# A vision tower's routed stage: lanes free with the table, tables sent sooner, outputs kept in fetched rows

## Chip, cores and metric

One Trainium2 chip, one of its cores. The time is the device time of one execution in microseconds; the kernel's figure is the median of three runs. In the profile PE is TensorE (PEld its weight loads), DVE VectorE, ACT ScalarE, POOL GpSimd, SP SyncE; L12 is line 12 of the kernel before.

## What is computed

Two layers of a small vision tower over 832 tokens (32 images, 26 positions, 256 features), all in float32. The change is in the last block, a mixture of 32 experts of which each token uses one, plus one shared expert:

```python
h = _L0_tok_ref(x, L0_tok_W)                    # patches, + class token
h = h + _L0_attn_ref(_layernorm(h), ...)
h = h + _L0_ffn_ref(_layernorm(h), ...)
h = h + _L1_attn_ref(_layernorm(h), ...)
h = h + _L1_ffn_ref(_layernorm(h), ...)         # the block that changes

# _L1_ffn_ref
shared_out = silu(x @ shared_gate_w) * (x @ shared_up_w) @ shared_down_w
logits = x @ gate_w
topk_ids = argmax(logits); scores = sigmoid(max(logits))
xs = x * scores
order = argsort(topk_ids)                       # tokens sorted by expert
g, u = grouped(xs[order], routed_gate_w), grouped(xs[order], routed_up_w)
d = grouped(silu(g) * u, routed_down_w)
return shared_out + d[argsort(order)]
```

## The kernel before

Every engine has its own hand-written stream, ordered by semaphores. Tokens are eight groups of 104. `x3T` holds the normalised tokens transposed (832 columns). The names that the change touches:

- **Memory.** One big tile, the arena, holds eight weight slots (one expert each, 1536 KB), behind them four *lanes*, behind them the shared expert's hidden values `hidT` and weights. `kz`, which also held `x3T`, and `zB`, which receives the shared silu, lie inside the area of the lanes. `cols3` is another tile (`qT`, `kT`, `xA` are its thirds, `quad` is all of it).
- **Routing.** VectorE derives from the logits the sorted slot of each token and two sets of records: *feeds* (which expert to load into which slot, and how many quads must have been copied before that slot is free) and *quads* (where the four weight sets of a quad lie, and how many loads must have landed). TensorE turns columns into rows for them (L607, `feeds_done`; L612 and L613, `table_done`), VectorE casts them into `table` (L1166 `feeds_table`, L1184 `table_ready`), and each engine loads its records into registers (`entry`, `weights_of`, `more_quads`), with bounds checked at run time.
- **Shared expert, up.** `shared_up(0..7)` on TensorE, a silu on ScalarE into `zB`, `hidden(0..7)` on VectorE into `hidT`; hand-placed between the routing steps. `shared_up(n)` waits for `hidden(n-2)`.
- **Tokens.** POOL scatters the scaled rows to `sorted_x` in memory (L1301). SP fetches windows of 128 rows back into `xw`: window 0, windows 1 and 2, windows 3 to 6 (`WINDOW_PARTS`); POOL fetches window 7.
- **Quads.** 128 sorted rows make a quad of four strips of 32 rows, each strip with one expert. In pass q TensorE does the gate and up strips of quad q (L628), the transpose of window q+1 (L620), some groups of `shared_down`, the down strips of quad q-1 (L641) and the transposes of quad q's hidden values (L634). ScalarE does the silu and evictions, VectorE the product (L1189) and the eviction of outputs (L1192). Before strips of quad q+1 can run, its weights are copied from slots into lanes: eight copies of 128x1024 on VectorE (L1195 to L1206), four on ScalarE (L824). Copies wait for `loaded`; SP waits for `copied_dve` and `copied_act` to reuse a slot.
- **Feeds.** SP keeps two loads in flight: it waits for the older one, raises `loaded`, waits until the slot is free, issues the next (L307).
- **Outputs.** `shared_rows(g)` adds the shared output to h, POOL stores it (L1317); when all eight groups are stored, POOL adds the quads' rows with indirect DMAs (L1310). The rows lie in a ring of four buffers `yw`, and VectorE waits for addition q-5 before it reuses one. `aim_static` computes the target rows of seven quads.
- **Last loop.** Passes 0 to 7 are written out. A loop of `more_quads` rounds (at least one; here one) does the down strips and addition of quad 7 and also the next quad, which is empty here. TensorE in it: down strips, wait for the window, transpose, gate strips, up strips, transposes. The end of the kernel waits for all engines.

## Time and profile before

| | |
|---|---|
| median of 3 runs | 354.5 us (353.39 to 355.84) |
| profiled execution | 352.22 us, span 350.4 us |
| TensorE, VectorE, ScalarE busy | 300.3, 206.3, 134.8 us |
| granted clock of TensorE, mean | 0.951 |
| expert loads after the routing | 14 of 1536 KB, issued 255.2 to 318.4 |
| stage from the first quad to the end | 263.8 to 350.4 |

The span runs from the first to the last instruction of the profiled execution; the execution's own time is 1.8 us more. All rows below give times from the start of the span. Busy shares are means over stages with different limits, so the stretch of the change is read by its waits, its chain and its timelines.

### The profile page before, as it was taken

How to read it: one execution, taken by the hardware profiler on the slowest of the kernel's cores; microseconds unless marked ns; L12 is line 12 of the kernel's file. 1: busy time of each engine (PE TensorE's matmuls, PEld its weight loads, DVE VectorE, ACT ScalarE, POOL GpSimd, SP SyncE). 2: the span in 40 equal slices, each digit the busy share in tenths (PEclk: the TensorE clock that was granted, in tenths of full speed). 3: DMA queues.
4: the chain of work that ended last, by engine and by line, in shares of the span. 5: the costliest groups of instructions: out<-in, count | busy, mean ns of one | idle time of the engine just before them, and what ended most of it. 6: DMA issues, size and time to landing. Idle time of an engine off the chain costs nothing.

```text
span 350.4 us, 6874 instructions
## 1 busy us (share of the span) xinstructions
PE 300.3 (86%) x2484; PEld 213.8 (61%) x2484; DVE 206.3 (59%) x589; ACT 134.8 (38%) x309; POOL 56.0 (16%) x73
## 2 busy tenths in 40 slices
PE   1996979388899999999975999989899999964958
PEld 1774548277899999998963766665454555421322
DVE  0454684433465665665266699948739867645653
ACT  1021242243242242242233466529147545615650
POOL 0111000100110110110000001111711210442350
PEclk9999899879999999999997799999999999996996
DMA  7999991003364264053597200000389996899231
GB/s 291 397 435 426 410 316 48 2 0 111 131 241 151 91 239 147 34 181 129 233 353 285 85 2 2 6 4 0 86 299 395 394 354 251 336 358 397 49 46 17
DMA packets 13115, 67.73 MB, mean 193 GB/s; under 512 B 1738, under 2 KB 7322, under 8 KB 8986
## 3 DMA queue, kind: packets, MB, share of 16 engines
q1 hardware_dynamic: 11050, 64.28, 47.9%
q0 software_dynamic: 2032, 3.02, 4.1%
q8 instruction: 20, 0.33, 0.4%
q14 instruction: 13, 0.11, 0.1%
HBM read 61.38 MB, written 5.91 MB: 192 GB/s over the span
## 4 chain that ended last, share of the span: by engine, by line
PE 64%; issue 11%; DMA 10%; DVE 8%; ACT 3%; SPq 1%; DVEq 1%; POOL 1%; ACTq 0%
PE P L340 17%; PE P L460 8%; PE P L448 8%; PE P L628 7%; DMA arena<-experts_dram 7%; PE P L374 4%; PE P L484 4%; PE P L510 3%; PE P L436 2%; PE P L641 2%; DMA vrow<-sorted_x 2%; DMA arena<-patches_dram 2%; PE P L525 1%; DVE arena L996 1%; PE P L535 1%
## 5 line engine op out<-in xcount | busy, mean ns | idle before, releaser
L340 PE MATMUL P<-arena 128*104 128x256 f32 x288 | 73.5, 395 | 9.4 <-DMA arena<-patches_dram 7.1
L340 PEld LDWEIGHTS P<-arena 128*104 128x104 f32 x288 | 47.4, 176 | 22.4 <-issue 8.3
L1290 POOL TENSOR_TENSOR rstd<-var,mhalf 104x1 f32<-104x1 f32 x40 | 21.9, 548 | 210.5 <-DVE var L919 210.5
L628 PE MATMUL P<-arena,cols 128*32 128x512 f32 x288 | 37.3, 664 | 11.1 <-ACT cols L849 9.1
L824 ACT ACTIVATE arena<-arena 128x1024 f32 x31 | 31.5, 1051 | 21.2 <-SPq L325 9.1
L460 PE MATMUL P<-arena 128*128 128x104 f32 x256 | 29.9, 275 | 2.4 <-ACT arena L764 2.4
L460 PEld LDWEIGHTS P<-arena 128*128 128x128 f32 x256 | 29.7, 192 | 3.1 <-issue 1.4
L448 PEld LDWEIGHTS P<-arena 128*128 128x128 f32 x256 | 29.8, 192 | 1.2 <-issue 0.7
L448 PE MATMUL P<-arena 128*128 128x104 f32 x256 | 29.8, 275 | 0.5 <-issue 0.5
L628 PEld LDWEIGHTS P<-arena,cols 128*32 128x32 f32 x288 | 9.1, 120 | 32.6 <-issue 19.1
L764 ACT ACTIVATE arena<-P,arena 128x104 f32<-128x104 f32 x64 | 17.0, 348 | 27.7 <-PE P L448 27.7
L577 PE MATMUL P<-arena 128*128 128x416 f32 x64 | 24.1, 522 | 2.0 <-DVE arena L1107 2.0
L749 ACT ACTIVATE arena<-P,arena 128x104 f32<-128x104 f32 x16 | 6.1, 433 | 43.2 <-PE P L427 43.2
L1310 POOL DMA_INDIRECT out_dram<-cols,target x8 | 16.5, 2058 | 23.5 <-DVE cols L1192 18.0
L925 DVE TENSOR_SCALAR arena<-h,mv,rstd 104x256 f32<-104x256 f32 x24 | 9.9, 413 | 16.0 <-POOL rstd L1290 16.0
L577 PEld LDWEIGHTS P<-arena 128*128 128x128 f32 x64 | 11.6, 190 | 11.4 <-issue 8.0
L641 PE MATMUL P<-arena,cols 128*32 128x256 f32 x192 | 15.4, 381 | 1.0 <-ACT cols L852 1.0
L484 PE MATMUL P<-arena 128*128 128x104 f32 x128 | 15.6, 275 | 0.6 <-DVE arena L1017 0.6
L484 PEld LDWEIGHTS P<-arena 128*128 128x128 f32 x128 | 15.0, 192 | 0.9 <-ACT arena L775 0.8
L1189 DVE TENSOR_TENSOR cols<-cols,P 128x512 f32<-128x512 f32 x9 | 6.2, 688 | 15.2 <-PE P L628 11.0
L724 ACT ACTIVATE cols<-P 128x104 f32<-128x104 f32 x16 | 4.2, 363 | 28.0 <-PE P L358 28.0
L917 DVE BATCH_NORM_STATS2 st<-h 104x6 f32<-104x256 f32 x32 | 13.7, 428 | 1.1
(200 smaller groups left out, 480.3 us busy)
## 6 DMA issues: line engine op xcount, KB each, us to landing
arena<-experts_dram SPq DMA_DIRECT2D x22, 1536.0 KB, 8.4
arena<-experts_dram SPq DMA_DIRECT2D x8, 2048.0 KB, 12.7
arena<-patches_dram SPq DMA_DIRECT2D x4, 624.0 KB, 6.3
sorted_x<-arena SPq DMA_DIRECT2D x1, 2056.0 KB, 35.2
arena<-shared_dram SPq DMA_DIRECT2D x1, 1536.0 KB, 32.4
arena<-w_dram SPq DMA_DIRECT2D x1, 1024.0 KB, 9.8
out_dram<-arena SPq DMA_DIRECT2D x1, 1024.0 KB, 33.7
out_dram<-h POOLq DMA_DIRECT2D x8, 104.0 KB, 4.9
```

Source lines behind the costliest of these rows:

```text
L340: last = mm(P[b][0:a.shape[1], col:col + D], a, rhs(c), start=(c == 0), stop=(c == chunks - 1))
L374: last = mm(bank(n % 4, HALF), w0_s[:, w, c, m * 128:(m + 1) * 128], xA[:, c, half * HALF:(half + 1) * HALF], start=(c == 0), stop=(c == D ...
L448: last = mm(bank(3 + m // 4, 4, GT)[:, m % 4, :], w[:, c, m * 128:(m + 1) * 128], xaT[:, c, :], start=(c == 0), stop=(c == DC - 1))
L460: last = mm(P[5][:, m * GT:(m + 1) * GT], w[:, c, m * 128:(m + 1) * 128], fhT[:, c, :], start=(c == 0), stop=(c == HC - 1))
L484: last = mm(bank(6, 4, GT)[:, 2 * w + m, :], w1_s[:, w, c, m * 128:(m + 1) * 128], x2T[:, c, :], start=(c == 0), stop=(c == DC - 1))
L577: last = mm(bank(b, HALF), w[:, c, m * 128:(m + 1) * 128], x3T[:, c, half * HALF:(half + 1) * HALF], start=(c == 0), stop=(c == DC - 1))
L628: last = mm(P[b][part, :], xT[:, c, part], weights(u)[:, c * INNER:(c + 1) * INNER], start=(c == 0), stop=(c == DC - 1), tile_position=(0, ...
L641: last = mm(P[3][part, 0:D], hT[:, c * 128 + STRIP * u:c * 128 + STRIP * (u + 1)], down_of(u, parity)[:, c * D:(c + 1) * D], start=(c == 0 ...
L764: A(fhT[:, m, :], bank(3 + m // 4, 4, GT)[:, m % 4, :], ACT.Gelu, bias=bcol_s[:, B1 + HC * g + m:B1 + HC * g + m + 1])\
L824: return A(to, third(where, n), ACT.Copy)
L1290: nc.gpsimd.tensor_tensor(rstd[:, :], var[:, :], mhalf[:, :], ALU.pow).then_inc(s["rstd_ready"], 1)
L1310: pool.indirect_dma_start(out, bass.IndirectOffsetOnAxis(ap=target[:, c:c + 1], axis=0), yw[:, c % YBUFS, :], None, compute_op=ALU.add)\
```

## The change

- `x3T` moves from `kz` to `qT`, `zB` into `quad`: the lanes are no longer touched by the shared up products. VectorE and ScalarE copy quad 0's weights as soon as the table is there, with `hidden(5)`, `(6)`, `(7)` placed between VectorE's copies.
- The feed records' product goes from behind `shared_up(4)` to behind `shared_up(3)`, the quad records' from behind `shared_up(5)` to behind `shared_up(4)`; `hidden(3)` goes behind the feed cast.
- Checks of record values at run time are dropped but for one per record.
- SP issues the second feed ahead of waiting for the scatters, and then the windows.
- `shared_down(0)` and `(1)` come before the quads, then one group in passes 1 and 2, two in passes 3 and 4 (before: group 0 ahead, group 1 in pass 0, two each in passes 1 to 3).
- Outputs are evicted into the fetched rows `xw` (quad 7: `y_last`); the ring `yw` and its waits go, the additions share a semaphore; `aim_static` covers eight quads and waits for window 7.
- The last loop: ScalarE copies two gate parts, VectorE five parts, ahead of the evictions; TensorE transposes the window ahead of the down strips; POOL fetches the first such window ahead of addition 6, and each further one behind the aim, which VectorE computes behind the product; the end waits for that window.
- `sorted_x` is one block of 128 rows longer.

Left out below: the buffer view `y_last`, the block count, the single semaphore `added`, and the checks' arguments in `entry`.

```diff
@@ -35,16 +35,19 @@
 WINDOW_PARTS = (0, 1, 3)
-SORTED = (MAX_QUADS + 1) * 128
+BLOCKS = MAX_QUADS + 2
+SORTED = BLOCKS * 128
...
 SPILLS = STILL + 1
-YBUFS = 4
+SHARED_FIRST = 2
+SHARED_AT = ((), (2,), (3,), (4, 5), (6, 7), (), (), ())
...
 XROW = D + 1
+IN_TABLE = "VectorE bounds each entry when it makes the table"
@@ -133,7 +136,8 @@
         x3 = vrow[:, :, 0:D]
-        oT = x3T = kz
+        oT = kz
+        x3T = qT
@@ -156,7 +160,7 @@
         spr = flat5[:, HALF + DC * GT:HALF + 2 * DC * GT].rearrange("p (c t) -> p c t", c=DC)
-        zB = flat5[:, 0:2 * HALF].rearrange("p (a n) -> p a n", a=2)
+        zB = quad[:, 0:2 * HALF].rearrange("p (a n) -> p a n", a=2)
@@ -226,8 +230,9 @@
             row = table[0:1, at:at + QUAD] if isinstance(q, int) else table[0:1, bass.ds(at, QUAD)]
-            _, found = nc.values_load_multi_w_load_instructions(row, engines=[engine.engine], min_val=0, max_val=(SLOTS - 1) * SLOT)
-            return found[LANES], found[0:LANES]
+            _, found = nc.values_load_multi_w_load_instructions(row, engines=[engine.engine], min_val=0, max_val=(SLOTS - 1) * SLOT,
+                                                                skip_runtime_bounds_check_because=IN_TABLE)
+            return nc.s_assert_within(found[LANES], 1, EXPERTS + 1), found[0:LANES]
@@ -312,10 +318,9 @@
             second = entry(1)
+            feed(second, 1)
             sp.wait_ge(xs_sent, 16 * GROUPS)
-            window(0)
-            feed(second, 1)
-            for i in range(1, len(WINDOW_PARTS)):
+            for i in range(len(WINDOW_PARTS)):
@@ -599,19 +604,19 @@
             last.then_inc(s["prefix_done"], 1)
-            for n in range(2, 5):
+            for n in range(2, 4):
                 shared_up(n)
...
             last.then_inc(s["feeds_done"], 1)
-            shared_up(5)
+            shared_up(4)
             pe.wait_ge(s["blocks_ready"], 1)
...
             mm(records[:, :, LANES], tcol[0:64, 1:2], ident[0:64, bass.ds(LANES - 1, 16, LANES)], start=True, stop=True).then_inc(s["table_done"], 1)
-            for n in range(6, 2 * IC):
+            for n in range(5, 2 * IC):
                 shared_up(n)
@@ -650,7 +655,8 @@
-            shared_down(0)
+            for g in range(SHARED_FIRST):
+                shared_down(g)
@@ -679,11 +685,8 @@
                     next_xt(q + 1)
-                if q == 0:
-                    shared_down(1)
-                elif q <= 3:
-                    shared_down(2 * q)
-                    shared_down(2 * q + 1)
+                for g in SHARED_AT[q]:
+                    shared_down(g)
                 if q >= 1:
@@ -697,13 +700,13 @@
             with pe.Fori(0, more) as i:
+                pe.wait_ge(l_window_in, 16 * (i + 2))
+                xt(STILL).then_inc(s["l_xt_done"], 1)
                 pe.wait_ge(s["l_hT_ready"], i + 1)
...
                 down_strips(STILL % 2).then_inc(s["l_dn_done"], 1)
-                pe.wait_ge(l_window_in, 16 * (i + 2))
-                xt(STILL).then_inc(s["l_xt_done"], 1)
                 pe.wait_ge(s["l_xT_ready"], i + 1)
@@ -854,7 +857,6 @@
-            act.wait_ge(s["hid_ready"], 2 * IC)
@@ -884,16 +886,16 @@
             with act.Fori(0, more) as i:
-                act.wait_ge(s["l_ht_done"], i + 1)
-                hT_evac().then_inc(s["l_hT_ready"], 1)
                 need, where = weights_of(act, i + (STILL + 1))
...
                 copy_third(where[3], 0, gate_of(3))
+                act.wait_ge(s["l_ht_done"], i + 1)
+                hT_evac().then_inc(s["l_hT_ready"], 1)
+                act.wait_ge(s["l_xt_done"], i + 2)
+                xT_evac().then_inc(s["l_xT_ready"], 1)
                 copy_third(where[2], 1, up_of(2)).then_inc(s["l_gatew_in"], 1)
                 act.wait_ge(s["l_dn_done"], i + 1)
-                act.wait_ge(s["l_xt_done"], i + 2)
-                xT_evac().then_inc(s["l_xT_ready"], 1)
                 copy_third(where[2], 2, down_of(2, STILL % 2)).then_inc(s["copied_act"], 1)
@@ -1158,12 +1160,11 @@
             V.tensor_scalar(table[:, T_FEEDS:T_FEEDS + 1], rounds, 1.0, None, ALU.max)
-            hidden(3)
...
             V.tensor_copy(table[:, 0:T_QUAD], P[5][0:1, 288:288 + T_QUAD]).then_inc(s["feeds_table"], 1)
+            hidden(3)
@@ -1182,14 +1183,12 @@
             V.tensor_copy(table[:, T_QUAD:NTABLE], P[4][0:1, 256:256 + 16 * QUAD]).then_inc(s["table_ready"], 1)
-            hidden(5)
-            hidden(6)
...
-            def y_evac(c):
-                return V.tensor_copy(yw[:, c, :], P[3][:, 0:D])
+            def y_evac(to):
+                return V.tensor_copy(to, P[3][:, 0:D])
@@ -1212,22 +1211,27 @@
                     dve.wait_ge(part, 16)
-                live7, ids7 = live[:, :, 0:STILL], xw[:, 0:STILL, D]
-                V.tensor_scalar(live7[:, 0, :], ids7, 0.0, None, ALU.is_gt)
-                link(V.tensor_tensor(live7[:, 1, :], ids7, route[:, C_SPILL1:C_SPILL1 + STILL], ALU.subtract))
-                link(V.tensor_tensor(live7[:, 1, :], live7[:, 1, :], live7[:, 0, :], ALU.mult))
-                V.tensor_tensor(target[:, 0:STILL], live7[:, 1, :], route[:, C_SPILL:C_SPILL + STILL], ALU.add).then_inc(s["aim_ready"], 1)
+                dve.wait_ge(l_window_in, 16)
+                dve.wait_ge(s["l_added"], 16)
+                ids8 = xw[:, 0:SPILLS, D]
+                V.tensor_scalar(live[:, 0, :], ids8, 0.0, None, ALU.is_gt)
+                link(V.tensor_tensor(live[:, 1, :], ids8, route[:, C_SPILL1:C_SPILL1 + SPILLS], ALU.subtract))
+                link(V.tensor_tensor(live[:, 1, :], live[:, 1, :], live[:, 0, :], ALU.mult))
+                V.tensor_tensor(target[:, :], live[:, 1, :], route[:, C_SPILL:C_SPILL + SPILLS], ALU.add).then_inc(s["aim_ready"], 1)
...
             need, where = weights_of(dve, 0)
-            hidden(7)
-            dve.wait_ge(s["hid_ready"], 2 * IC)
             dve.wait_ge(s["loaded"], need)
+            dve.wait_ge(s["xs_scaled"], GROUPS)
             copy_gate(where).then_inc(s["gatew_in"], 1)
+            hidden(5)
             copy_up(where).then_inc(s["upw_in"], 1)
-            shared_rows(0)
+            hidden(6)
...
             need, where = weights_of(dve, 1)
+            hidden(7)
+            for g in range(SHARED_FIRST):
+                shared_rows(g)
@@ -1241,15 +1245,11 @@
                     aim_static()
-                    shared_rows(1)
-                elif q <= 3:
-                    shared_rows(2 * q)
-                    shared_rows(2 * q + 1)
+                for g in SHARED_AT[q]:
+                    shared_rows(g)
...
                     dve.wait_ge(s["dn_done"], q)
-                    if q > YBUFS:
-                        dve.wait_ge(added[q - 1 - YBUFS], 16)
-                    y_evac((q - 1) % YBUFS).then_inc(s["y_ready"], 1)
+                    y_evac(xw[:, q - 1, 0:D]).then_inc(s["y_ready"], 1)
@@ -1258,26 +1258,25 @@
             nc.vector.nop().then_inc(s["l_turn"], 1)
-            dve.wait_ge(added[STILL - YBUFS], 16)
             with dve.Fori(0, more) as i:
-                dve.wait_ge(s["l_added"], 16 * (i + 1))
-                dve.wait_ge(l_window_in, 16 * (i + 1))
+                need, where = weights_of(dve, i + (STILL + 1))
+                dve.wait_ge(s["loaded"], need)
+                copy_gate(where)
+                copy_up(where).then_inc(s["l_gatew_in"], 1)
+                dve.wait_ge(s["l_dn_done"], i + 1)
+                y_evac(y_last).then_inc(s["l_y_ready"], 1)
+                copy_down(where, STILL % 2).then_inc(s["copied_dve"], 1)
+                dve.wait_ge(s["l_sgate_ready"], i + 1)
+                dve.wait_ge(s["l_up_done"], i + 1)
+                mul().then_inc(s["l_hw_ready"], 1)
+                dve.wait_ge(l_window_in, 16 * (i + 2))
                 ids = xw[:, STILL, D:XROW]
...
                 dve.wait_ge(s["l_aimed"], i + 1)
+                dve.wait_ge(s["l_added"], 16 * (i + 2))
                 V.scalar_tensor_tensor(target[:, STILL:], live[:, 1, STILL:], live[:, 0, STILL:], route[:, C_SPILL + STILL:C_SPILL + SPILLS],
                                        ALU.mult, ALU.add).then_inc(s["l_aim_ready"], 1)
-                need, where = weights_of(dve, i + (STILL + 1))
-                dve.wait_ge(s["l_dn_done"], i + 1)
-                y_evac(STILL % YBUFS).then_inc(s["l_y_ready"], 1)
-                dve.wait_ge(s["loaded"], need)
-                copy_gate(where)
-                copy_up(where).then_inc(s["l_gatew_in"], 1)
-                copy_down(where, STILL % 2).then_inc(s["copied_dve"], 1)
-                dve.wait_ge(s["l_sgate_ready"], i + 1)
-                dve.wait_ge(s["l_up_done"], i + 1)
-                mul().then_inc(s["l_hw_ready"], 1)
@@ -1304,10 +1303,12 @@
-                pool.dma_start(xw[:, STILL, :], sorted_x[bass.ds(r * 128, 128), :]).then_inc(l_window_in, 16)
+                rows_r = slice(r * 128, (r + 1) * 128) if isinstance(r, int) else bass.ds(r * 128, 128)
+                pool.dma_start(xw[:, STILL, :], sorted_x[rows_r, :]).then_inc(l_window_in, 16)
...
             def add_rows(c, done):
-                pool.indirect_dma_start(out, bass.IndirectOffsetOnAxis(ap=target[:, c:c + 1], axis=0), yw[:, c % YBUFS, :], None, compute_op=ALU.add)\
+                y = xw[:, c, 0:D] if c < STILL else y_last
+                pool.indirect_dma_start(out, bass.IndirectOffsetOnAxis(ap=target[:, c:c + 1], axis=0), y, None, compute_op=ALU.add)\
@@ -1320,21 +1321,23 @@
                     pool.wait_ge(s["stored"], 16 * GROUPS)
+                if r == STILL - 1:
+                    pool.wait_ge(s["l_xt_done"], 1)
+                    window(STILL + 1)
                 pool.wait_ge(s["y_ready"], r + 1)
-                add_rows(r, added[r])
+                add_rows(r, added)
...
             with pool.Fori(0, more) as i:
-                pool.wait_ge(s["l_aim_ready"], i + 1)
-                pool.wait_ge(s["l_xt_done"], i + 1)
                 pool.wait_ge(s["l_turn"], i + 1)
-                window(i + (STILL + 1))
                 pool.wait_ge(s["l_y_ready"], i + 2)
...
                 add_rows(STILL, s["l_added"])
-            for r in range(STILL):
-                pool.wait_ge(added[r], 16)
-            pool.wait_ge(l_window_in, 16 * (more + 1))
+                pool.wait_ge(s["l_xt_done"], i + 2)
+                pool.wait_ge(s["l_aim_ready"], i + 1)
+                window(i + (STILL + 2))
+            pool.wait_ge(added, 16 * STILL)
+            pool.wait_ge(l_window_in, 16 * (more + 2))
             pool.wait_ge(s["l_added"], 16 * (more + 1))
```

## Rows read from the trace of the kernel before

**Rows 1.** The page, part 1: busy us, share of the span, instructions.
```profile
PE 300.3 (86%) x2484; PEld 213.8 (61%) x2484; DVE 206.3 (59%) x589; ACT 134.8 (38%) x309; POOL 56.0 (16%) x73
```

**Rows 2.** Waits, 240 to 352: waiter <- awaited: total us, times, longest.
```profile
ACT arena L824 <- SPq L325: 9.1, 1, 9.1
```

**Rows 3.** The chain that ended last, from 225: start, us, engine and line.
```profile
257.03 5.72 DMA vrow<-sorted_x
...
273.94 3.45 PE P L340 x16
...
301.44 7.44 DMA arena<-experts_dram
...
318.42 8.14 DMA arena<-experts_dram
...
329.03 3.64 PE P L628 x32
...
348.75 0.70 DVE cols L1189
```

**Rows 4.** DVE timeline, 247 to 254: start, us, engine, line, operation.
```profile
247.41 0.15 DVE L1154 TENSOR_SCALAR tcol<-own 128x1 f32<-128x1 f32 x1
...
251.48 0.25 DVE L1166 CAST table<-P 1x96 int32<-1x96 f32 x1 [1.82 <-PE P L607]
...
253.52 0.15 DVE L1177 TENSOR_SCALAR tcol<-own 128x1 f32<-128x1 f32 x1
```

**Rows 5.** PE timeline, 248 to 290: shared products, tables, first strips of quads.
```profile
248.12 3.06 PE L577 MATMUL P<-arena 128*128 128x416 f32 x8 [1.15 <-DVE arena L1107]
...
254.36 0.27 PE L612 MATMUL P<-ident,tcol 64*1 64x64 f32 x2
...
260.31 1.89 PE L340 MATMUL P<-arena 128*104 128x256 f32 x8
...
263.83 3.64 PE L628 MATMUL P<-arena,cols 128*32 128x512 f32 x32 [0.53 <-ACT cols L849]
...
269.93 3.64 PE L628 MATMUL P<-arena,cols 128*32 128x512 f32 x32
...
289.62 3.64 PE L628 MATMUL P<-arena,cols 128*32 128x512 f32 x32
```

**Rows 6.** SP timeline: issue of the first fed expert.
```profile
255.16 0.36 SPq L307 DMA_DIRECT2D arena<-experts_dram  x1
```

**Rows 7.** Windows: stretch, length, busy of PE, PEld, DVE, ACT, POOL; clock, DMA, GB/s.
```profile
270.00:284.00 14.00, 14.00 (x122) 6.59 (x123) 11.05 (x24) 7.96 (x12) 2.75 (x3) 1.00 0.98 388
301.40:326.60 25.20, 16.93 (x166) 5.97 (x162) 12.87 (x21) 10.99 (x15) 10.03 (x5) 0.86 0.96 341
341.00:349.00 8.00, 6.51 (x32) 1.39 (x32) 3.08 (x6) 1.08 (x2) 0.53 (x1) 0.57 0.16 18
```

**Rows 8.** DVE timeline, 299 to 301.3: last weight copy of quad 4.
```profile
300.56 0.69 DVE L1206 COPY arena<-arena 128x1024 f32 x1
```

**Rows 9.** ACT, DVE, POOL, PE timelines of the last pass, 334 to 340.
```profile
335.17 0.60 ACT L852 ACTIVATE cols<-P 128x512 f32<-128x512 f32 x1 [3.33 <-PE P L634]
337.12 2.95 ACT L824 ACTIVATE arena<-arena 128x1024 f32 x3 [1.35 <-issue]
...
336.80 0.61 POOL L1307 DMA_DIRECT2D vrow<-sorted_x  x1
...
338.35 0.42 DVE L1192 COPY cols<-P 128x256 f32<-128x256 f32 x1 [2.31 <-PE P L641]
...
339.68 0.44 PE L620 MATMUL P<-ident,vrow 128*128 128x128 f32 x2 [1.73 <-DMA vrow<-sorted_x]
```

**Rows 10.** Lines L1310, L1338, L82: count, min/median/max ns, first and last start us.
```profile
L1310 POOL DMA_INDIRECT out_dram<-cols,target x8: 1546/1850/2946, 303.6 to 339.6; - x8
...
L1338 POOLq EVENT_SEMAPHORE  x1: 17/17/17, 344.3 to 344.3; - x1
...
L82 POOLq DRAIN  x1: 2273/2273/2273, 344.5 to 344.5; - x1
```

13 lines of the change are left out of this document (7 added, 6 removed).

## Prediction

> **What bounds the kernel now.** I read the page first: TensorE is busy for 86% of the span, VectorE for 59% [rows 1]. That is an average, so the place of the change decides, which is everything after 244 us. The waits of that stretch come next: ScalarE stood 9.1 us before a weight copy, released by SP's line 325, which is the landing of expert weights [rows 2]. The chain of waits orders it. From the first window (landed 262.75) until quad 4 the chain is TensorE, pass after pass; from 301.44 it is weight loads, two always in flight, until the last landed at 326.56; from quad 7's gate strips (329.03) it is a tail that ends 0.9 us after the last product of VectorE [rows 3]. So there are three regimes: TensorE, then DMA, then a tail of dependencies. The profiled execution's span is 350.4 us in 352.2 us; the three timed runs have a median of 354.5. I add up against the span and carry the difference to the median.
>
> I number the feeds (expert weights loaded after the routing) F0 to F13 and call the first gate strips of quad q "start of q".
>
> **1. Tables sooner: SP gets its table 2.3 us earlier.** VectorE has the columns ready at 247.56 (L1154), yet the cast that frees SP starts at 251.48 [rows 4], because TensorE queues the product behind the fifth shared_up, which begins 248.12 [rows 5]. Now the product comes after the fourth, at about 247.6, and VectorE reaches the cast after its short operations at about 249.2, with hidden(3) out of the way. The first feed was issued at 255.16 [rows 6]; it goes to 252.8, perhaps 251.5 with the runtime bounds checks gone.
>
> **2. What TensorE pays for it: +0.6 us.** The quad records now stand before shared_up(5). Their inputs need hidden(3) (0.5) and the ten operations that took 251.7 to 253.67 [rows 4], 2.0 us: ready at 249.4 + 0.5 + 2.0 = 251.9. The fifth product set ends 251.2 [rows 5], so TensorE waits 0.7 and is spared nothing: the record products (254.36) only change place. The first shared_down begins at 260.9 in place of 260.31.
>
> **3. Two shared_down ahead of the quads.** One group costs 3.45 / 2 = 1.73 us [rows 3]. The start of quad 0 was 263.83 after one group and a wait for the window of 0.6 us [rows 5]. Now 260.9 + 3.45 + 0.95 (transpose and eviction, 262.88 to 263.83) = 265.3. The window is issued behind two feeds instead of one: 3.28 MB at 388 GB/s [rows 7] is 8.5 us, from about 253.5 (F0's issue plus latency): 262.5 to 263.5, before 264.4 where TensorE first wants it. Cover of one microsecond; each later microsecond would be paid in full. The copies of quad 0, freed from waiting for the last shared product, are finished by then and hide behind TensorE: worth nothing alone.
>
> **4. The passes.** Quad 0 took 263.83 to 269.93 = 6.10 with one group, quads 1 and 2 together 19.69, so 9.85 each with two groups [rows 5]. Without its group quad 0 would take 4.37, but quad 1's gate strips then wait for VectorE: product 3.65 after the start, 0.7 for it [rows 3], two copies of 0.6: 5.65. So 1.3 us of the 1.73 is lost. Quads 1 and 2 carry one group each: 8.1 us (VectorE needs about 7). Start of quad 3: 265.3 + 5.65 + 8.1 + 8.1 = 287.15, against 289.62: **-2.5 us**. Quads 3 and 4 pay the rest back (9.85 each, quad 4 before 6.4), but from there weights set the pace.
>
> **5. The feeds.** A slot comes free when a quad's copies are over. F9 was issued at 301.44, right after quad 4's last copy ended at 301.25 [rows 3, 8], 11.6 after the start of quad 3; now about 298.9. Earlier feeds start 2.3 us sooner but wait for the copies of quads 2 and 3 instead, so the lead of part 1 is used up there. From F9 on it is bandwidth: 25.2 us to F13's landing at 341 GB/s = 8.6 MB, five feeds of 1.57 MB and five row additions [rows 7]. Two stores of output rows (104 KB each) now fall into this stretch, since groups 6 and 7 move from quad 3 to quad 4: 0.2 MB, +0.6 us. F13 lands at about 324.7, quad 7 starts at T = 327.1 instead of 329.03: **-1.9 us**. The row additions start about 7 us later (they wait for all eight stores), still five of them before F13. I cost the later start at nothing because outputs stay in xw and nobody waits for a buffer back; at about 2 us each they are through before quad 6's rows are ready. Without that cover each would cost VectorE's next eviction 2 us. Fewer bounds checks on VectorE and ScalarE lie beside waits.
>
> **6. The tail, from T (327.1 now, 329.03 before; before it lasted 21.4).** Before: hT evicted at T+6.1, three weight copies of ScalarE took 2.95 [rows 9], down strips at T+7.0, y evicted T+9.3, five copies by VectorE, gate strips T+13.1, their product T+19.7, end T+21.4. Now ScalarE loads the record (0.9) and makes two copies (2.0) ahead of the eviction: T+9.0. Down strips T+9.85 to T+11.8, hidden behind nothing: +2.85. VectorE's five copies run meanwhile (T+7.5 to T+10.6), so the gate strips follow at T+11.8 rather than T+13.1.
> Gate and up strips last 3.64 us [rows 3] at the full clock (2.4 GHz) and 6.5 in the stretch 341 to 349, where the mean grant was 0.57, nearly all of it the 1.2 GHz level [rows 7]. TensorE now stands 3.9 us but for two transposes; before it stood 3.1 like that and the grant fell. I take 55% for the low one. VectorE's product ends at T+16.2 or T+19.1.
> **The new end.** The aim of the last window now stands behind that product and behind the landed addition; POOL's window transfer stands behind the aim; the final waits stand behind the transfer. Nothing else is queued there. The addition: y evicted T+11.9, issue T+13.1, landing 4.7 later (339.6 to 344.3 [rows 10]): T+17.8. Aim T+18.3 or T+19.4. Issue to arrival 2.9 (336.80 to 339.68 [rows 9]): T+21.4 or T+22.5. POOL's closing DRAIN lasted 2.27 [rows 10]: end T+23.9 to T+25.0 with 0.2 to leave. Bounds of the drain: 0.5 (as on the other engines) if it is time of the earlier additions, 2.3 if fixed; I take 2.3, the only row of POOL. Tail 24.6 against 21.4: **+3.2 us** (+0.9 at the lowest).
> Two rules weighed. POOL writes descriptors in 1.5 to 2.95 us [rows 10], the long ones while VectorE copies. The Trainium skill, GPSIMD Engine Reference, section Key points, says that it shares its memory interfaces with VectorE when that runs in a 2-port mode. By that rule the last addition, now beside copy_down, may take 1.0 us longer, and the full-clock tail 25.1 instead of 24.1. The transfer's 2.9 us is from a row; the Trainium skill, DMA: Bandwidth & Descriptors, section Anatomy of one DMA, gives about 2.0 plus the bytes at 436 GB/s, 2.3 here, an estimate that would make the sum 0.6 smaller.
>
> **Sum.** 350.4 - 1.9 + 3.2 = 351.7 us of span; +1.3 on the median gives **355.8 us**, 0.4% above now.
>
> **Rivals.**
> (a) *The window lands late* (slower). If the feeds flow at 325 GB/s beside the last scatters, 3.28 MB take 10.1 us and the bounds checks save nothing: it lands at 266 or later, quad 0 starts 2.4 us later and so does all behind it: 358.2. It decides once the window lands after 264.4. For it: SP's transfers land in order; the window, issued 1.9 us behind F0, took 5.7 us for 128 KB [rows 3, 6]. Against: the scatters end by 256. Chance 0.12.
> (b) *The gain stays in the feeds.* The last five take 27.7 instead of 25.8, because additions and stores crowd together after 310, and F13 lands where it did: 350.4 + 3.2, 357.7. For it: 341 GB/s with additions against 388 without [rows 7]. Chance 0.15, a third of it beyond 1%.
> (c) *The tail is short*: the drain runs beside other waits, the clock is full: T+22.3, 354.5 - 1.9 + 0.9 = 353.5. Chance 0.18.
> (d) *The feeds gain more* (faster). With the early additions gone, F9 to F12 run at 388 GB/s: 8.8 MB take 22.7, F13 lands at 321.6, T = 324.0, span 350.4 - 5.0 + 3.2 = 348.6, 352.7; with a short drain besides 350.9. Chance 0.15.
> That the sooner tables do nothing for the end is already in the sum (part 5). Left for the forecast: 0.40.
>
> A measurement of this kernel tells about 1% from no change, 3.5 us. Slower than 358.0: (a), a third of (b) and 0.03 of the forecast with everything at its upper bound, 0.20. Faster than 351.0: half of (d) and a third of (c) where the passes also lose less than part 4 says, with rounding 0.15. Between: 0.65. The range reaches from the short tail with more feed gain (351.3) to (a) with the low clock (358.8).
>
> **What would show it.** Right: first feed issued near 252 to 253; quad 0 starting later (265) but quad 3 earlier (287); F9 near 299; quad 7 near 327; down strips of the last pass 2.9 later from T than before; POOL's window transfer as the last thing but the drain. Wrong if F13 lands at 326 or after, if the grant or the drain shifts the tail by more than 2 us, or if quad 0 waits for its window.

## The result and the profile after

The changed kernel takes 356.27 us, the median of 19 runs (352.87 to 360.37); the kernel before, on the same chip, takes 354.5 us (19 runs, 352.06 to 356.12). The ratio is 1.0047, 95% interval 1.0028 to 1.0066: no change by the 1% that a measurement of this kernel can tell, with a small loss of 1 to 2.3 us inside it. The forecast of 355.8 us and its likeliest class held. How the two large terms behind it came out is the better lesson, so I go through them. In what follows a ratio takes only the executions within about 1.5% of their kernel's fastest, while medians and traces take all, and the traces of e9 and e11 are of executions that their ratios leave out.

The profiled execution took 355.21 us with a span of 353.5. Part 1 of its page answers to [rows 1]:

```profile
PE 302.6 (86%) x2484; PEld 217.1 (61%) x2484; DVE 206.4 (58%) x589; ACT 135.1 (38%) x309; POOL 54.9 (16%) x74
```

Nothing moved there: a gain and a loss of some 3 us each don't show in shares of a span. Before the two traces are compared, one thing far ahead of the change has to be taken out. Here are the same stretches in both (windows: stretch, length, busy of PE, PEld, DVE, ACT, POOL, then granted clock, DMA share, GB/s), first of before, then of after:

```profile
50.00:56.00 6.00, 4.39 (x20) 3.41 (x20) 3.47 (x9) 2.35 (x2) 0.00 (x0) 1.00 0.66 212
66.00:80.00 14.00, 8.14 (x49) 7.24 (x49) 5.87 (x19) 4.65 (x13) 2.19 (x4) 0.76 0.00 1
```

```profile
50.00:56.00 6.00, 3.88 (x11) 3.21 (x12) 3.10 (x8) 2.35 (x2) 0.00 (x0) 0.72 0.93 238
66.00:80.00 14.00, 8.28 (x39) 6.96 (x38) 5.39 (x17) 2.56 (x6) 1.65 (x3) 0.63 0.00 0
```

The profiled execution of after was granted the lower clock once more, and once for longer, in a part that no edit touches, and reaches the first scatter of rows at 246.43 us where before reached it at 243.70. That the change isn't the cause is seen in e3 and e7 below: e3 carries all edits ahead of this scatter, e7 all but those of the tables, and they reach it at 243.57 and 243.58. So I count from that scatter, called S0, and from T, the start of quad 7's gate strips. From S0 to T before took 85.3 us and after takes 82.0; from T to the end before took 21.4 and after takes 25.1. Gain 3.4, loss 3.7, and 2.7 of clock ahead of both make the 3.1 by which the two spans differ; the medians differ by 1.8, and they mostly stand at one mean clock (0.938 to 0.944 in 16 of 19 executions of after, 0.942 in most of those of before whose clock is on record), while the profiled one of before had 0.951.

Timeline of after, TensorE: the first gate strips of quads 0 to 7, which answer to [rows 5]:

```profile
267.52 3.64 PE L633 MATMUL P<-arena,cols 128*32 128x512 f32 x32 [0.47 <-ACT cols L852]
273.30 3.68 PE L633 MATMUL P<-arena,cols 128*32 128x512 f32 x32 [0.60 <-issue]
281.46 3.64 PE L633 MATMUL P<-arena,cols 128*32 128x512 f32 x32
289.58 3.64 PE L633 MATMUL P<-arena,cols 128*32 128x512 f32 x32
299.42 3.64 PE L633 MATMUL P<-arena,cols 128*32 128x512 f32 x32
309.26 3.64 PE L633 MATMUL P<-arena,cols 128*32 128x512 f32 x32
319.39 6.25 PE L633 MATMUL P<-arena,cols 128*32 128x512 f32 x32 [3.67 <-ACT cols L852]
...
328.38 3.64 PE L633 MATMUL P<-arena,cols 128*32 128x512 f32 x32
```

Quad 3 starts at the same time on the clock as before (289.62) although S0 is 2.7 later: that is the gain of the passes. And from its chain of waits, the pieces that answer to [rows 3]:

```profile
301.39 6.95 DMA arena<-experts_dram
308.69 8.23 DMA arena<-experts_dram
...
319.39 6.25 PE P L633 x32
...
328.45 3.57 PE P L633 x32
332.02 1.77 PE P L646 x32
334.54 0.55 ACTq L233
336.42 1.04 ACT arena L827
338.18 3.56 PE P L646 x32
342.28 0.56 POOL rstd L1334
343.00 4.06 DMA out_dram<-cols,target
348.21 0.61 POOL vrow L1307
```

The regimes are those of before up to quad 6, but not up to T. Before, the chain went through the landing of F13, which TensorE waited for ahead of quad 7 (0.30 us of idle time). Here the last landing on it is F11's, at 316.92; quad 6 waits for the copies behind it (the 3.67 above), its gate and up strips take 6.25 us at a mean grant of 0.58 instead of 3.64 at the full one, and quad 7 starts behind them with no wait. F13 had landed at 325.7, 2.7 us ahead of T. Against S0 quad 6 starts 3.9 us sooner than before, and its pass takes 9.0 us instead of 8.4. Behind T the chain is a new one: ScalarE's copy (L827), the down strips, the row addition, the aim, POOL's window. The gate strips of the last pass aren't on it any more. The end of it, from the operations of line 85:

```profile
L85 POOLq COMPARE_BRANCH  x1: 41/41/41, 350.7 to 350.7; - x1
L85 POOLq DRAIN  x1: 2357/2357/2357, 350.9 to 350.9; - x1
```

### The profile page after: what moved, and what is told of

Same layout as the page of the kernel before. It is cut to its first block, busy times and chain, and to the rows that moved or that the text cites. A ratio compares the mean times of both kernels' runs of the same rounds, so it can differ in the third digit from the quotient of the medians.

```text
span 353.5 us, 6670 instructions
## 1 busy us (share of the span) xinstructions
PE 302.6 (86%) x2484; PEld 217.1 (61%) x2484; DVE 206.4 (58%) x589; ACT 135.1 (38%) x309; POOL 54.9 (16%) x74
## 4 chain that ended last, share of the span: by engine, by line
PE 71%; DVE 10%; DMA 7%; issue 4%; ACT 4%; POOL 1%; ACTq 1%; DVEq 0%; SPq 0%; POOLq 0%
PE P L345 17%; PE P L453 8%; PE P L465 8%; PE P L633 7%; PE P L582 5%; DMA arena<-experts_dram 4%; PE P L379 4%; PE P L646 4%; PE P L489 4%; PE P L441 2%; PE P L515 2%; PE P L530 2%; DMA arena<-patches_dram 2%; DVE arena L998 1%; DMA out_dram<-cols,target 1%
## 5 line engine op out<-in xcount | busy, mean ns | idle before, releaser
L345 PE MATMUL P<-arena 128*104 128x256 f32 x288 | 74.3, 398 | 9.5 <-DMA arena<-patches_dram 7.2
L633 PE MATMUL P<-arena,cols 128*32 128x512 f32 x288 | 35.6, 637 | 4.7 <-ACT cols L852 4.1
L827 ACT ACTIVATE arena<-arena 128x1024 f32 x31 | 31.6, 1051 | 18.4 <-PE P L646 5.9
L465 PE MATMUL P<-arena 128*128 128x104 f32 x256 | 29.9, 275 | 2.4 <-ACT arena L767 2.4
L465 PEld LDWEIGHTS P<-arena 128*128 128x128 f32 x256 | 29.7, 192 | 3.1 <-issue 1.4
L453 PEld LDWEIGHTS P<-arena 128*128 128x128 f32 x256 | 30.8, 197 | 1.3 <-issue 0.7
L453 PE MATMUL P<-arena 128*128 128x104 f32 x256 | 30.6, 279 | 0.5 <-issue 0.5
L582 PE MATMUL P<-cols,arena 128*128 128x416 f32 x64 | 23.8, 520 | 1.0 <-DVE arena L1109 1.0
L646 PE MATMUL P<-arena,cols 128*32 128x256 f32 x192 | 17.0, 401 | 2.8 <-ACT cols L855 2.8
L582 PEld LDWEIGHTS P<-cols,arena 128*128 128x128 f32 x64 | 11.7, 190 | 10.1 <-issue 8.3
L489 PE MATMUL P<-arena 128*128 128x104 f32 x128 | 15.6, 275 | 0.6 <-DVE arena L1019 0.6
L489 PEld LDWEIGHTS P<-arena 128*128 128x128 f32 x128 | 15.0, 192 | 0.9 <-ACT arena L778 0.8
L1311 POOL DMA_INDIRECT out_dram<-vrow,target x7 | 12.1, 1732 | 14.8 <-DVE vrow L1191 7.4
L998 DVE TENSOR_SCALAR arena<-P,arena 128x104 f32<-128x104 f32 x16 | 4.5, 321 | 17.0 <-PE P L465 17.0
```

What stands on the lines that cost most here:

```text
L345: last = mm(P[b][0:a.shape[1], col:col + D], a, rhs(c), start=(c == 0), stop=(c == chunks - 1))
L453: last = mm(bank(3 + m // 4, 4, GT)[:, m % 4, :], w[:, c, m * 128:(m + 1) * 128], xaT[:, c, :], start=(c == 0), stop=(c == DC - 1))
L465: last = mm(P[5][:, m * GT:(m + 1) * GT], w[:, c, m * 128:(m + 1) * 128], fhT[:, c, :], start=(c == 0), stop=(c == HC - 1))
L489: last = mm(bank(6, 4, GT)[:, 2 * w + m, :], w1_s[:, w, c, m * 128:(m + 1) * 128], x2T[:, c, :], start=(c == 0), stop=(c == DC - 1))
L582: last = mm(bank(b, HALF), w[:, c, m * 128:(m + 1) * 128], x3T[:, c, half * HALF:(half + 1) * HALF], start=(c == 0), stop=(c == DC - 1))
L633: last = mm(P[b][part, :], xT[:, c, part], weights(u)[:, c * INNER:(c + 1) * INNER], start=(c == 0), stop=(c == DC - 1), tile_position=(0, ...
```

## The experiments

Each figure comes from 4 (e12) to 12 executions, compared with 23 or 29 of the kernel before on the same chip. "T" and "tail" are from the profiled execution, counted as above; the time against the changed kernel is the difference of the two ratios, times 354.5.

| run | median us | ratio to before (95%) | S0 to T | tail |
|---|---|---|---|---|
| before | 354.5 | 1 | 85.3 | 21.4 |
| after | 356.27 | 1.0047 (1.0028 to 1.0066) | 82.0 | 25.1 |
| e1_old_loop | 351.06 | 0.990 (0.9854 to 0.9945) | 81.9 | 19.9 |
| e2_new_loop | 360.07 | 1.018 (1.0141 to 1.0219) | 85.5 | 25.6 |
| e3_old_shared | 358.9 | 1.0154 (1.0112 to 1.0196) | 85.0 | 25.4 |
| e4_window_first | 356.51 | 1.0058 (1.0028 to 1.0089) | 83.4 | 25.2 |
| e5_evict_first | 353.73 | 0.9995 (0.9969 to 1.002) | 83.9 | 22.3 |
| e6_no_last_window | 353.26 | 0.9924 (0.9879 to 0.997) | 83.0 | 22.4 |
| e7_old_tables | 356.94 | 1.0089 (1.0046 to 1.0132) | 84.2 | 25.0 |
| e8_checks | 356.84 | 1.0061 (1.0028 to 1.0094) | 82.0 | 25.6 |
| e9_late_shared | 354.36 | 0.9883 (0.983 to 0.9936) | 81.8 | 24.5 |
| e10_copies_first | 349.89 | 0.9855 (0.9797 to 0.9913) | 82.6 | 19.0 |
| e11_both | 353.79 | 0.9906 (0.987 to 0.9942) | 80.6 | 25.3 |
| e12_half_feeds | 349.75 | 0.9879 (0.9843 to 0.9916) | 75.6 | 25.0 |

### The loop alone, taken away and added

e1_old_loop is the changed kernel with the last pass (the loop) of before, on TensorE, ScalarE, VectorE and POOL.

```
 ACT loop:  wait l_ht_done; hT_evac()          # first, as before
            copy_third(where[2], 0, gate_of(2)); copy_third(where[3], 0, gate_of(3)) ...
 DVE loop:  aim; y_evac(y_last); copy_gate; copy_up    # aim and y first
 POOL loop: wait aim; window; wait y; add_rows          # no window behind the addition
```

> The changed kernel with the last loop of before (TensorE, ScalarE, VectorE and POOL parts, seven-quad aim, no early window). Theory A: the change gains about 3 us up to quad 7 and gives them back in the tail. Then the tail, from quad 7's gate strips to the end, is 20 to 21.5 us instead of 25.1, and the kernel is 3 to 4.5 us faster than the changed one: 352 to 353.5, about 2 us below before. Theory B (the loss is not in the tail but in chance grants of TensorE's clock upstream): the tail shrinks, but the time stays at 355.5 to 357.

Measured: 351.06 us, ratio 0.990, so 5.2 us under the changed kernel and about 1 below the range I had given; T is where the change puts it (81.9), the tail is 19.9. e2_new_loop is the reverse: the kernel before with only the new loop.

> The kernel before with only the last loop of the changed one (copies ahead of the evictions, window fetched ahead of addition 6, closing window behind the aim, eight-quad aim). Theory A: slower than before by 3 to 4 us, 357.5 to 359; the tail from quad 7's gate strips is 24.5 to 26 us, everything before quad 7 as before. Theory B: within 1 us of before.

Measured: 360.07 us, 1.8% above before and above the range I had given, with T as before (85.5) and a tail of 25.6. By the times the new loop costs 5.2 us (e1) and 6.4 us (e2), and what stands ahead of it gains 3.5 and 4.7. By the tails of the traces it costs 5.2 and 4.2. So the two agree on the sign and on some 4 to 6 us; why e2 is 2 us longer than its tail explains is open. One part of the cost is POOL's closing. Operations of line 85 in e1:

```profile
L85 POOLq DRAIN  x1: 2273/2273/2273, 343.3 to 343.3; - x1
...
L85 PEldq DRAIN  x1: 438/438/438, 347.3 to 347.3; - x1
```

The same 2.3 us as in after, but here begun at 343.3 and over before TensorE closes; in after it begins at 350.9 and the span ends with it.

### What in the loop costs it

e6_no_last_window leaves out POOL's fetch of the next window inside the loop and the wait for it (no row of the output depends on it in this data).

```
                 pool.wait_ge(s["l_aim_ready"], i + 1)
-                window(i + (STILL + 2))
...
-            pool.wait_ge(l_window_in, 16 * (more + 2))
+            pool.wait_ge(l_window_in, 32)
```

> The changed kernel without the last loop's own window fetch and without the end's wait for it (with these inputs the loop runs once and that window is never used; it leaves that transfer out). Theory A: the closing window costs what stands behind the product: 2.9 us of transfer; POOL's closing drain stays at 2.3 us. The end comes 2.5 to 3 us earlier, 353.3 to 354. Rival: the transfer lies beside the closing of the other engines, and less than 1 us is gained.

Measured: 353.26 us. That is 4.4 us under the changed kernel by the ratios and 2.6 by the medians, each set against before on its own chip; the tail is 22.4 instead of 25.1, 2.7 us shorter, within the 2.5 to 3 that I had expected. POOL's closing started at 348.8 and still ended last. e5_evict_first puts ScalarE's eviction of hT ahead of its two copies.

```
             with act.Fori(0, more) as i:
+                act.wait_ge(s["l_ht_done"], i + 1)
+                hT_evac().then_inc(s["l_hT_ready"], 1)
                 ...
                 copy_third(where[3], 0, gate_of(3))
-                act.wait_ge(s["l_ht_done"], i + 1)
-                hT_evac().then_inc(s["l_hT_ready"], 1)
```

> The changed kernel, with one thing of the loop's order put back: ScalarE evicts the hidden table (hT) ahead of its two gate copies instead of behind them. Computes the reference in full. Theory (the prediction's tail sum: the three copies of 2.95 us on ScalarE stand between the sigmoid and the eviction of hT, and put the loop's down strips late): counted from T, the start of the strips of quad 7, hT is evicted at about T+6.2 instead of T+9.0, the down strips start at about T+7.0 instead of T+9.8, the last row addition lands some 3 us sooner, and the end comes at about T+21.5 instead of T+25.1; time 3 to 3.6 us under the changed kernel. The gate strips of the loop come later than before relative to the down strips, at about T+10.7 to T+13, which costs nothing as long as their own window is not the last thing. Rival (the closing chain through the loop's own window sets the end whatever the down strips do): down strips early, but the time within 1 us of the changed kernel. If so the loop's late end would be the window's wait and the closing of POOL, not the copies.

Measured: 353.73 us, 1.8 us under the changed kernel, where 3 to 3.6 were expected. The timeline of its last pass (T is 330.12) says where the rest stayed:

```profile
336.26 0.60 ACT L855 ACTIVATE cols<-P 128x512 f32<-128x512 f32 x1 [3.32 <-PE P L639]
337.09 0.41 PE L646 MATMUL P<-arena,cols 128*32 128x256 f32 x2 [0.35 <-ACT cols L855]
340.06 0.68 DVE L1200 COPY arena<-arena 128x1024 f32 x1
340.67 0.41 DVE L1191 COPY cols<-P 128x256 f32<-128x256 f32 x1
341.89 1.82 POOL L1311 DMA_INDIRECT out_dram<-cols,target  x1 [0.17 <-issue]
347.10 0.62 POOL L1307 DMA_DIRECT2D vrow<-sorted_x  x1 [3.39 <-DVE target L1278]
```

hT is out at T+6.1 and the down strips start at T+7.0, both as expected. But y is evicted at T+10.55, not at T+9.3 as before: it stands behind VectorE's five copies, which end at T+10.6. Of the 4.1 us by which the change has y later than before, counted from T, 1.2 are left, in VectorE's queue, where the new order has the same fault. The tail fell by 2.8 and 1.9 of it came back in S0 to T, by the spread of the weight loads that is told below.

e10_copies_first asks whether VectorE's new order is the good half: the loop of before, with its copies ahead of y.

```
+                dve.wait_ge(s["loaded"], need)
+                copy_gate(where); copy_up(where)...
                 dve.wait_ge(s["l_dn_done"], i + 1)
                 y_evac(y_last).then_inc(s["l_y_ready"], 1)
-                dve.wait_ge(s["loaded"], need)
-                copy_gate(where); copy_up(where)...
```

> The changed kernel with the loop of before (as e1_old_loop), and VectorE's copies of the loop's weights ahead of the eviction of y instead of behind it. Computes the reference in full. Theory (VectorE stands idle until the down strips end, and the gate strips of the loop wait for its copies): the gate strips start at about T+10.7 instead of T+12.7 and the end is 0.5 to 2 us sooner than e1's. Rival (the end hangs on the down strips' row addition, not on the gate strips): y is evicted later by up to 1 us and the time is the same or 0.5 us above e1's.

Measured: tail 19.0 against e1's 19.9; 349.89 against 351.06 us, a difference within the intervals. The gate strips started at T+11.8, sooner than e1's T+12.7 but not at T+10.7:

```profile
336.60 1.00 POOL L1305 DMA_DIRECT2D vrow<-sorted_x  x1
...
339.67 0.44 PE L625 MATMUL P<-ident,vrow 128*128 128x128 f32 x2 [1.90 <-DMA vrow<-sorted_x]
...
340.66 5.34 PE L633 MATMUL P<-arena,cols 128*32 128x512 f32 x32 [0.55 <-ACT cols L852]
```

The copies were no longer the last thing awaited; the loop's own window was, landed 3.0 us after POOL issued it. This is the lowest ratio of the study, 0.9855 (0.9797 to 0.9913), though the intervals of e1, e9, e11 and e12 overlap with it. It is faster than both before and after, with the schedule of the change and the loop of before.

### The schedule ahead of T

e3_old_shared is the changed kernel with the shared down groups where before had them.

```
-SHARED_FIRST = 2
-SHARED_AT = ((), (2,), (3,), (4, 5), (6, 7), (), (), ())
+SHARED_FIRST = 1
+SHARED_AT = ((1,), (2, 3), (4, 5), (6, 7), (), (), (), ())
```

> The changed kernel with the shared down products placed as before: one group ahead, one in pass 0, two each in passes 1 to 3. Theory A: TensorE's passes set the pace up to quad 4, so quad 3 starts 2.5 to 3 us later than in the changed kernel, F9 is issued as much later, and the time is 2.5 to 3 us longer: 358.5 to 359.5. Theory C (the feeds' earlier start is what helps): quad 7 starts within 1 us of the changed kernel and the time is the same.

Measured: 358.9 us, 3.8 us over the changed kernel; S0 to T 85.0 instead of 82.0. Its quad 3 starts 46.2 us behind S0 (after: 43.15) and F9 is issued 58.0 behind it (after: 55.0). All of the gain of 3 us is there.

e7_old_tables puts the first table product and its cast back behind shared_up(4) and hidden(3).

```
-            for n in range(2, 4):
+            for n in range(2, 5):
                 shared_up(n)
...
             V.tensor_copy(table[:, 0:T_QUAD], ...).then_inc(s["feeds_table"], 1)
-            hidden(3)
```

> The changed kernel, with the records product and the table's cast put back behind shared_up(4) and hidden(3) where they stood before; the schedule of shared_down, the addition rows and the loop stay as changed. Computes the reference in full. Theory (the prediction's own sum: the earlier table frees the first feed by 2.3 us, but TensorE's stretch up to the strips is bounded by its own work and by the feeds from quad 3 on): cast and first feed about 2.3 us later against the first scatter, the windows are issued about as late or up to 2 us later, strips of quad 0 at most 1 us later, T within 0.5 to 1 us, time 0 to 1 us above the changed kernel. Rival (the early table is worth its full 2.3 us, since all feeds move with it): T and the time 2 to 2.5 us later. Second rival (the early feeds delay the scatters' landing, so the earlier table buys nothing): windows issued about 4 us after the last scatter instead of 7, and T the same to 0.3 us.

Measured: F0 is issued 9.6 us behind S0 (after: 7.9), quad 0 starts 22.2 behind it (after: 21.1), F9 56.1 (after: 55.0), T 84.2; 356.94 us, 1.5 us over the changed kernel with 1.6 to each side. So the sooner tables give 1.1 us at quad 0 and F9, a little above my bound; the 1.2 more at T lie inside the spread of the weight loads. Of the 1.1, TensorE's own order is 0.65 (the shared down products start 17.4 behind S0 instead of 16.8). The rest is window 0, which landed 21.2 behind S0 and kept TensorE waiting:

```profile
264.89 0.41 PE L625 MATMUL P<-ident,vrow 128*128 128x128 f32 x2 [0.25 <-DMA vrow<-sorted_x]
```

e8_checks puts the runtime bounds checks of the quads' records back.

```
-            _, found = ...(row, ..., max_val=(SLOTS - 1) * SLOT, skip_runtime_bounds_check_because=IN_TABLE)
-            return nc.s_assert_within(found[LANES], 1, EXPERTS + 1), found[0:LANES]
+            _, found = ...(row, ..., max_val=(SLOTS - 1) * SLOT)
+            return found[LANES], found[0:LANES]
```

> The changed kernel, with the runtime bounds checks of weights_of (the engines' loads of a quad's record: its free marker and lanes) put back on VectorE and ScalarE; nothing else is undone. Computes the reference in full. Theory (the prediction: fewer bounds checks lie beside waits and are worth nothing): strips of quads 1 to 5 within 0.3 us, T within 0.5, but in the loop the record's load on ScalarE stands ahead of its copies, so that hT may be evicted up to 0.8 us later and the end with it: time 0 to 1 us above the changed kernel. Rival (the record loads stand ahead of each quad's copies, which free the slots for the feeds): each quad's copies end 0.5 to 1 us later, F9 and F11 are issued later, T and the time 1.5 to 3 us later.

Measured: S0 to T 82.0, tail 25.6, 0.5 us over the changed kernel and within its interval. Costed at nothing ahead of T, and worth nothing there. In the loop the checks stand ahead of ScalarE's copies: hT was evicted at T+9.9 instead of T+9.0, as expected.

### Scatters, feeds and the window

e4_window_first has SP send window 0 ahead of the second feed.

```
             feed(entry(0), 0)
             second = entry(1)
-            feed(second, 1)
             sp.wait_ge(xs_sent, 16 * GROUPS)
+            window(0)
+            feed(second, 1)
```

> The changed kernel, with SP sending window 0 ahead of the second feed F1 (order: F0, wait for the scatters, window 0, F1, windows 1 and 2). Computes the reference in full. Theory (feeds that flow beside the scatters delay the scatters' landing, but window 0 has about 1 us of cover, so it costs nothing): the wait for the scatters ends 4.5 to 5.5 us after the last scatter's issue instead of 7.1, window 0 is issued 1.5 to 3 us sooner; strips of quad 0 start where they did against the first scatter, within 0.3 us. F1 starts 4 us later, and if the feeds are one train that the DMA paces from F0 to F13, the last feed lands up to 2 us later and the time is 0 to 2 us above the changed kernel. Rival (the late window holds up quad 0 after all): quad 0 starts 1 us sooner and the time falls by 1 us. Rival (nothing of the train's early part matters): time as the changed kernel within 0.5 us.

e12_half_feeds cuts each of the 14 feeds to its first half; the other half of each slot keeps older weights, so half of the fed weights is left out.

```
-                sp.dma_start(feeds_s[:, bass.ds(at, SLOT)], experts1[bass.ds(e, 1)]...)
+                sp.dma_start(feeds_s[:, bass.ds(at, SLOT // 2)], experts1[bass.ds(e, 1), :, 0:SLOT // 2]...)
```

> The changed kernel, with each of the 14 feeds after the routing cut to its first half (6 KB of 12 KB a partition); the other half of a slot keeps older weights, so part of the expert weights is left out. It takes the DMA's load from the feeds and leaves every instruction in its place. Theory (from quad 5 on the landing of the feeds is what starts a quad; up to quad 5 TensorE is): strips of quads 0 to 5 start as in the changed kernel to 0.5 us, quad 6 about 5.8 us after quad 5 (instead of 10.1), quad 7 about 6 us after quad 6 (instead of 9.0), T about 7 us sooner, tail the same 24.5 to 25, time about 349. It would also show whether the scatters' late landing (7.1 us after the last issue) is the feeds' doing: about 5 instead. Rival (TensorE and VectorE between them bound the passes, and the feeds only keep up): T sooner by less than 2 us. Rival for the scatters (they are late by themselves): still 7 us.

What POOL waited for ahead of its first window transfer, in after, in e4, in e12 and in e10, one fence each (timeline; the wait in brackets is that for the scatters' landing):

```profile
263.08 0.62 POOL L1314 DMA_DIRECT2D vrow<-sorted_x  x1 [6.39 <-DMA sorted_x<-vrow,slot_i]
```

```profile
262.38 0.62 POOL L1315 DMA_DIRECT2D vrow<-sorted_x  x1 [5.19 <-DMA sorted_x<-vrow,slot_i]
```

```profile
261.20 0.62 POOL L1314 DMA_DIRECT2D vrow<-sorted_x  x1 [4.14 <-DMA sorted_x<-vrow,slot_i]
```

```profile
264.05 0.62 POOL L1312 DMA_DIRECT2D vrow<-sorted_x  x1 [7.51 <-DMA sorted_x<-vrow,slot_i]
```

In e10, whose code up to here is that of the changed kernel, SP happened to issue F1 1.6 us behind F0 instead of 3.6 (why is open), and the scatters landed later still. From the issue of the last scatter to that of window 0 it was 4.0 to 4.1 us in before and e2 (F0 alone, issued after the last scatter), 4.9 with two half feeds (e12), 5.9 with one (e4), 5.9 to 8.3 with two issued 3.6 us apart (e3, e6, e1, after, e11, e8; after 7.1), and 7.9 to 8.6 with two issued 1.6 us apart (e7, e10, e5, e9). More feed bytes beside the scatters, later landing: the mechanism of rival (a) is real. With the tables where the change has them it never decided (in e7 it cost some 0.4 us). Quad 0 starts 21.1 us behind S0 in after, e4 and e10 alike, with window 0 issued at 15.2 (e4), 16.4 (after) or 17.5 (e10) us behind S0, because TensorE is busy with the second shared group until then. The time of e4 is that of the changed kernel within 0.4 us.

e12 also settles who sets T. Its strips of quads 5, 6 and 7, on TensorE's timeline:

```profile
309.65 3.64 PE L633 MATMUL P<-arena,cols 128*32 128x512 f32 x32
316.04 3.64 PE L633 MATMUL P<-arena,cols 128*32 128x512 f32 x32
322.43 3.64 PE L633 MATMUL P<-arena,cols 128*32 128x512 f32 x32
```

Up to quad 5 nothing moves against S0 (62.8 us in both); then the passes take 6.4 us each instead of 10.1 and 9.0, with no wait. T comes 6.3 us sooner, the tail stays at 25.0, the time falls by 6.0. So TensorE sets the pace to quad 5 and the landing of the weights from there; the rival that TensorE and VectorE bound the passes falls. The 6.3 us have two parts: 3.7 are the wait ahead of quad 6 that is gone, and 2.6 are quad 6's strips, at the full grant here (3.64 us) and at a mean of 0.58 in after (6.25). In every kernel with whole feeds TensorE waited 1.9 to 8.3 us ahead of those strips, and they took 5.3 to 6.5.

e9_late_shared and e11_both try to use that: two shared groups ahead, then none, (2,), (3,), (4, 5), (6, 7) behind quads 2 to 5, once with e1's loop, once with e10's.

```
-SHARED_AT = ((), (2,), (3,), (4, 5), (6, 7), (), (), ())
+SHARED_AT = ((), (), (2,), (3,), (4, 5), (6, 7), (), ())
```

> The changed kernel with the loop of before (as e1_old_loop), and one quad's delay of the shared down groups: none behind quad 1, two products (instead of none) from behind quad 2 on, so that quads 0 to 2 run with fewer other products between them. Computes the reference in full. Theory (from quad 3 on the feeds' DMA, freed by the copies of quad 3, sets the pace; what stands ahead of quad 3 on TensorE therefore costs its full length): the strips of quad 3 start about 1.8 us sooner against the first scatter, F9 is issued sooner by 1.5 to 3.5 us, T is 2 to 3.5 us sooner, time 348 to 349.5 against e1's 351.1. Rival (DMA-bound already from the first feed, so that TensorE's order ahead of quad 3 is free): quad 3 sooner, F9 not, T within 0.5 us, time as e1. Second rival (the shared products are pushed into the stretch in which TensorE has no slack): T as e1 or up to 2 us later.

> The loop of before with VectorE's copies ahead of the eviction of y (as e10_copies_first), and the shared down groups one quad later (as e9_late_shared). Computes the reference in full. Theory (the feeds from F0 to F13 are one train of 71 to 75 us that the DMA paces, so TensorE's schedule ahead of quad 5 no longer matters): quad 5 starts 3 us sooner than in e10, quad 6 within 0.5 us, T the same; time as e10 (349.9) within 0.7 us. Rival (the later groups do free slots sooner and e9 only missed by chance): T 1 to 2 us sooner, 348 to 349.

Measured: ratios 0.9883 against e1's 0.990, and 0.9906 against e10's 0.9855; no gain. By the medians, each over that of before on its chip, e9 is at 1.002 and e1 at 0.991, e11 at 0.997 and e10 at 0.989: a loss. Quad 5 starts 3.4 us (e9) and 3.3 us (e11) sooner behind S0, as intended, quad 6 only 0.4 and 1.9, T 0.2 and 2.0. In e9 F9 went out 1.5 us sooner and the last feed landed at the same time. In the trace of e11 the tail is 25.3 instead of 19.0, three times what T gained. POOL in e9's timeline shows how:

```profile
320.54 2.85 POOL L1316 DMA_DIRECT2D out_dram<-h  x2 [15.22 <-DVE h L1209]
327.77 2.08 POOL L1309 DMA_INDIRECT out_dram<-vrow,target  x1 [4.38 <-DMA out_dram<-h]
...
340.20 1.71 POOL L1309 DMA_INDIRECT out_dram<-vrow,target  x1 [0.30 <-issue]
341.25 1.29 POOL L1305 DMA_DIRECT2D vrow<-sorted_x  x1
```

Groups 6 and 7 are now evicted behind VectorE's copies of quad 6, and those wait for the weights that land at 316.7. The last two stores of shared rows thus go out from 320.5 on instead of 307.3 (e1), all seven row additions queue on POOL from 327.8 to 341.9, and the loop's window stands behind them: TensorE waited 7.6 us for it and its gate strips began at 346.2 instead of 340.8. I had named lateness on TensorE as the rival, not on POOL. In these two traces, then, the change's own placement, (6, 7) behind quad 4, is the last that keeps the additions off the loop. Both are of long executions (354.6 and 355.5 us), as five of seven of e9 (352.8 to 355.4) and seven of twelve of e11 (352.6 to 356.1) are; the others took 349.1 to 350.9, and no trace shows whether their tails are as long.

## Why the prediction was right, and where its terms were off

**Tables (part 1).** Against S0 the cast came 2.4 us sooner (predicted 2.3) and F0 3.5 (1.1 of checks and loads on top; I had left that open). **TensorE (parts 2, 3).** The shared down products start 0.2 us later against S0 (predicted +0.6), quad 0 1.0 later (predicted +1.5). The window's landing was right for the wrong reason: I put it behind two feeds in SP's queue, but SP waited for the scatters to land, and it was the feeds that made them late. The cover of about a microsecond held: the window landed 19.4 us behind S0 and TensorE wanted it at 20.2. In e8 it landed at 20.1 and quad 0 still started at 21.1; in e7 it was late, as told. Two of my numbers in these parts don't come out of their own terms: the addends of quad 0's pass make 5.55, not 5.65, and the window of rival (a), 10.1 us from 253.5 and up to 1.3 later without the saving of checks, lands at 265 at the latest, not at 266.

**Passes (part 4).** 5.8, 8.2, 8.1, 9.8, 9.8 us against 5.65, 8.1, 8.1, 9.85, 9.85. Quad 3 gained 2.8 against S0 (predicted 2.5). e3 confirms it from the other side, 3.0. **Feeds (part 5).** F9 gained 2.8 (predicted 2.5). From F9 to the landing of F13 took 24.3 us in this execution; the step said 25.8. The stretch's windows answer to [rows 7]:

```profile
301.40:325.70 24.30, 20.63 (x173) 8.47 (x166) 13.22 (x22) 11.11 (x15) 9.78 (x7) 0.86 0.98 352
338.20:341.80 3.60, 3.60 (x36) 2.27 (x40) 0.84 (x3) 0.97 (x2) 0.00 (x0) 0.53 0.02 5
```

352 GB/s instead of 341, in spite of the two more stores. But this is one draw, and T wasn't set by it. I had T 2.4 us behind the landing of F13; here quad 6's strips at the lower grant, a term I didn't have, kept TensorE busy until then. In after, e1, e8 and e9 there was no wait ahead of quad 7, and T is 81.8 to 82.0; where F13 came later (e4, e5, e6, e7, e10) TensorE waited 0.4 to 1.2 us for its copies, and T is 82.6 to 84.2. In the seven profiled executions whose order from F9 on is that of the change (after, e1, e5, e6, e7, e8, e10) the same stretch took 24.3, 24.2, 26.5, 25.5, 25.7, 24.0 and 25.2: mean 25.1, which is what before took. So the 0.6 for the stores doesn't show, and a term of 25 us at the DMA's limit carries a spread of more than 2 us from one execution to the next, as large as the gain I wanted to read. Over the six of them that have the sooner tables S0 to T is 82.6 on average: a gain of 2.7 against 85.3, between the 1.9 predicted and the 3.4 of this trace.

**Tail (part 6).** Predicted 24.6, measured 25.1, and 25.0 to 25.6 in every run with the new loop and the change's window. In its pieces: hT at T+9.0 and down strips at T+9.8, as predicted. The down strips then took 3.56 us instead of 1.93, at 1.2 GHz (second line of the fence above: grant 0.53), so y was evicted at T+13.4 instead of T+11.9. I had the fall of the grant and what precedes it, TensorE standing for a few microseconds, but put it on the gate strips one place later; there the grant was nearly full (0.96), and they had left the path. (Ahead of the gate strips of before TensorE stood 3.7 us but for the transposes, not the 3.1 that I read.) The row addition landed 4.1 us after its issue, not 4.7. The aim ran at T+18.8 (predicted T+18.3 or T+19.4):

```profile
347.15 0.22 DVE L1278 SCALAR_TENSOR_TENSOR target<-live,cols 128x1 int32<-128x1 f32 x1 [0.97 <-DMA out_dram<-cols,target]
348.21 0.62 POOL L1307 DMA_DIRECT2D vrow<-sorted_x  x1 [3.38 <-DVE target L1278]
```

POOL needed 0.85 us from the aim's end to the transfer, where I had 0.2, and the transfer was over within 2.5 us of its issue (2.4 in e3, e4, e5 and e7, whose traces have its landing), where I had 2.9. By the fixed part and the bytes in the Trainium skill, DMA: Bandwidth & Descriptors, section Anatomy of one DMA, the estimate is 2.3; on this transfer it is nearer than my row was, and on the window of e10 (3.0) my row is. The closing of POOL was 2.36 us and on the path: the bound of 0.5 is out, since it took 2.27 begun 0.25 us behind the last addition's landing (e1), 2.27 begun 1.1 behind it (e6) and 2.36 begun 3.9 behind it (after). The Trainium skill, GPSIMD Engine Reference, section Key points, says that POOL shares its memory interfaces with VectorE and contends with VectorE's 2-port modes. The 1.0 us that I took from rows for the last addition beside VectorE's copies didn't come about: it took 1.82 us with copies running beside it, while additions with none beside them took 1.55 to 1.60. The trace agrees with the direction, and the size is 0.25. It is larger on POOL's stores of shared rows: the first two of after took 1.97 and 1.96 us with copies beside them, the other four 0.55.

**Sum.** With the averages, -2.7 + 3.9 = +1.2 us against the measured +1.0 to +2.3. I predicted -1.9 + 3.2 = +1.3. Both terms were undersized by 0.7 to 0.8 and the errors cancelled; the range wasn't needed, but that was partly luck. Both figures of before, 85.3 and 21.4, are of one trace. In it the closing gate strips took 6.51 us at the lower grant; e1, with the same loop, had them in 5.34 and a tail of 19.9.

**Rivals.** (a), the window late: that feeds beside the scatters make it late is shown, and it bound only in e7, by some 0.4 us. (b), the gain stays in the feeds: e5 came nearest (F9 to F13 26.5 of its 27.7), but not the average. (c), the tail is short: excluded by POOL's closing in every run. (d), the feeds gain more: the trace of after looks like half of it (S0 to T 3.4 sooner, between 1.9 and 5.0), and the other executions show that this was the spread.

**Still open.** Why F1 follows F0 by 1.6 us in some profiled executions and by 3.6 in others with the same code. And why an addition beside copies takes 2.95 us at one time and 1.83 at another. It isn't where the rows lie: e2, which keeps the old ring, has 1.83 in both places where before has 2.95, and e3 and e6, which take the rows from the window's tile, have 2.95 once each.

## What to carry to other kernels

Copying weights ahead of an eviction is good only on an engine for which nobody waits at that moment: here the order on ScalarE alone put the down strips 2.8 us later, and taking that back won 2.8 us of the tail and left a stall of 1.2 us in VectorE's queue. Count a closing chain to its very last instruction, a queue's closing included, since an early finish of POOL hides 2.3 us that a late one pays in full. And where a stretch runs at the DMA's limit, take its length from several executions before you credit an edit with 1 or 2 us of it.

## What the hardware showed that I had not expected

- Scatters by row index land later when large loads flow beside them: 4.0 to 4.1 us from the last issue when the first load starts only behind them, 4.9 with two of 0.79 MB, 5.9 with one of 1.57 MB, 5.9 to 8.6 with two.
- POOL's closing takes 2.27 to 2.36 us in every run, whatever ran before it, against 0.43 to 0.48 on TensorE and ScalarE and 0.06 or 0.50 on VectorE.
- The stretch at the lower grant moved with the order of the last pass: over the down strips in after (3.56 us at 0.53), over the gate strips in e1 and e10 (5.34 us each, against 3.64 at the full grant), over neither in e5 (gate strips 3.64). With the order of after it reached into the gate strips in e3, e4 and e6 (4.7 to 4.9 us).
- A wait for weights costs more than its length: behind the 3.7 us that TensorE stood ahead of quad 6 in after, its gate and up strips took 6.25 us at a mean grant of 0.58, and 3.64 in e12, where it didn't stand.
